# Score units 8 to 12 of a batch issued sooner and in pairs, with the keys' transposes one step earlier

## What is computed

```python
scores = jnp.einsum('bqhd,bkhd->bhqk', q, k) * scale
scores = jnp.where(mask, scores, jnp.finfo(scores.dtype).min)
attn = jax.nn.softmax(scores, axis=-1)
out = jnp.einsum('bhqk,bkhd->bqhd', attn, v).reshape(B, S, N_HEADS * V_DIM)
return out @ Wo
```

## Time and profile before

| | |
|---|---|
| median of 3 runs | 791.5 us (791.44 to 791.93) |
| profiled execution | 791.67 us, span 789.9 us, so 1.77 us lie around the span |
| PE busy | 778.6 us, 99% of the span |
| PE weight loads busy | 711.5 us, 90% |
| DVE busy | 681.7 us, 86% |
| ACT busy | 524.5 us, 66% |
| POOL busy | 479.5 us, 61% |

### The profile page before, as it was taken

One profiled execution on the slowest core, in us unless ns is written; L12 is line 12 of the kernel. 1 busy time (PEld: TensorE's weight loads), 2 busy tenths in 40 slices (PEclk: granted clock), 3 DMA queues, 4 the chain that ended last, 5 costly groups with the idle time before them and its releaser, 6 DMA issues.

```text
span 789.9 us, 23152 instructions
## 1 busy us (share of the span) xinstructions
PE 778.6 (99%) x7976; PEld 711.5 (90%) x7976; DVE 681.7 (86%) x2616; ACT 524.5 (66%) x1612; POOL 479.5 (61%) x1278
## 2 busy tenths in 40 slices
PE   9999999999999999999999999999999999999988
PEld 7889889888889889898998989899898998989867
DVE  6998897888688899989898998989989898998885
ACT  5554454445555787777767777677777867777682
POOL 6880202202236696776867768686776867768673
PEclk9999999999999999999999999999999999999999
DMA  8600220000002222322222322223222222322220
GB/s 302 253 2 2 62 82 27 1 1 1 1 15 52 40 46 52 61 54 36 48 46 50 64 39 50 40 46 55 56 55 35 48 46 49 63 39 53 34 52 28
DMA packets 101334, 41.15 MB, mean 52 GB/s; under 512 B 91744, under 2 KB 98400, under 8 KB 100576
## 3 DMA queue, kind: packets, MB, share of 16 engines
q1 hardware_dynamic: 98896, 38.89, 22.1%
q10 hardware_dynamic: 2320, 0.79, 0.4%
HBM read 14.47 MB, written 4.19 MB: 24 GB/s over the span
## 4 chain that ended last, share of the span: by engine, by line
PE 92%; DVE 4%; ACT 1%; POOL 1%; issue 1%; ACTq 0%; POOLq 0%; DVEq 0%
PE bank L549 63%; PE bank L773 11%; PE bank L795 8%; PE bank L766 3%; PE bank L629 2%; PE bank L815 1%; PE bank L566 1%; DVE SM L1608 1%; PE bank L681 1%; ACT SM L1065 1%; DVE PT L1631 1%; PE bank L641 1%; PE bank L655 1%; POOL SM L2051 1%; PE bank L700 0%
## 5 line engine op out<-in xcount | busy, mean ns | idle before, releaser
L1065 ACT ACTIVATE SM<-SM,stb 128x224 f32<-128x224 f32 (+7 forms) x512 | 207.2, 407 | 62.7 <-DVE stb L1608 58.2
L2051 POOL TENSOR_SCALAR SM<-SM,stb 128x224 f32<-128x224 f32 (+7 forms) x512 | 195.2, 396 | 67.5 <-DVE stb L1615 66.1
L549 PE MATMUL bank<-yh,wq_lo 128*128 128x256 f32 x512 | 150.6, 294 | 0.0
L549 PE MATMUL bank<-yh,wq_hi 128*128 128x256 f32 x512 | 144.7, 283 | 0.0
L549 PE MATMUL bank<-yl,wq_hi 128*128 128x256 f32 x512 | 144.6, 282 | 0.0
L773 PE MATMUL bank<-KT,QT 128*128 128x192 f32 (+4 forms) x640 | 120.9, 327 | 1.7 <-DVE stb L1608 1.7
L1608 DVE CUSTOM_DVE_ANT_0 SM<-bank,CONST 128x224 f32<-128x224 f32 (+3 forms) x320 | 97.2, 348 | 23.3 <-PE bank L773 20.9
L1631 DVE STREAM_TRANSPOSE PT<-SM 128x128 f32<-128x128 f32 (+2 forms) x232 | 99.7, 462 | 16.7 <-PE bank L795 16.7
L773 PEld LDWEIGHTS bank<-KT,QT 128*128 128x128 f32 x640 | 97.5, 190 | 5.3 <-DVE stb L1608 3.6
L549 PEld LDWEIGHTS bank<-yh,wq_lo 128*128 128x128 f32 x512 | 97.1, 190 | 1.4
L549 PEld LDWEIGHTS bank<-yh,wq_hi 128*128 128x128 f32 x512 | 97.1, 190 | 0.0
(11 more groups left out here) (229 smaller groups left out, 2068.9 us busy)
## 6 DMA issues: line engine op xcount, KB each, us to landing
QT<-QA SPq DMA_DIRECT2D x240, 64.0 KB, 2.1
PT<-KV SPq DMA_DIRECT2D x256, 16.0 KB, 1.8
out<-fo SPq DMA_DIRECT2D x32, 128.0 KB, 2.0
X<-in_x SPq DMA_DIRECT2D x7, 512.0 KB, 11.5
stage<-in_wqn SPq DMA_DIRECT2D x2, 1024.0 KB, 5.3
stage<-in_wo SPq DMA_DIRECT2D x2, 1024.0 KB, 4.9
stage<-in_w1t SPq DMA_DIRECT2D x4, 256.0 KB, 5.0
stage<-in_w2t SPq DMA_DIRECT2D x2, 512.0 KB, 6.2
```

The source lines that it names most:

```text
L549: i = e.matmul(dst, a, b, start=(first and j == 0), stop=(last and j == 2), skip_group_check=skip)
L1065: i = e.activation(M[:, at], M[:, at], ACT.Exp, bias=S[:, 0, j:j + 1], scale=-1.0, accum_out=S[:, 1, j:j + 1])
L2051: i = e.tensor_scalar(P[:, at], P[:, at], S[:, 2, j:j + 1], 1.0, ALU.mult, ALU.mult)
```

## The change

TK_AT becomes 7, with TK_FIRST = 8 kept for batch 0. So `l1_tk` and `keys` run one step sooner in batches 1 to 14, and tk moves in the list of shared banks: it now stands ahead of the second output product instead of behind the gate product.

A new function, `scores_at`, gives the units that PE issues at a step. In batches 1 to 14: S7 and S8 at m = 7, S9 and S10 at m = 8, S11 and S12 at m = 9 (in batch 14 only S11), and then nothing at m = 0, 1, 2 of the next batch (in the last batch nothing at 0 and 1). All units still go out in the same order, to the same two banks, with the same waits. `l1_misc` moves ahead of the scores of its step in batches 1 and later. DVE, ACT and POOL keep their steps, but for `keys`.

```diff
-TURN_AT, TM_AT, TK_AT, LORA_AT, MISC_AT = 6, 6, 8, 8, (8, 9)
+TURN_AT, TM_AT, TK_AT, TK_FIRST, LORA_AT, MISC_AT = 6, 6, 7, 8, 8, (8, 9)
+def scores_at(n):
+    if not 0 <= n < TOTAL:
+        return ()
+    b, m = divmod(n, UNITS)
+    if b and m < 3 and b > 1 and (b < NB - 1 or m < 2):
+        return ()
+    if b and b < NB - 1 and m > 6:
+        return {7: (n, n + 1), 8: (n + 1, n + 2), 9: (n + 2, n + 3) if b < NB - 2 else (n + 2,)}[m]
+    if n and with_next(n - 1):
+        return ()
+    return (n, n + 1) if with_next(n) else (n,)
+def tk_of(n):
+    b, m = divmod(n, UNITS)
+    return b + 1 if m == (TK_AT if b else TK_FIRST) and b + 1 < NB else None
 # shared_bank_order
-        if m == TK_AT and b + 1 < NB:
-            js.append(("tk", b + 1))
+        if tk_of(n):
+            js.append(("tk", tk_of(n)))
 # PE's program
-                if n < TOTAL and not (n and with_next(n - 1)):
-                    l1_s(n)
-                    if with_next(n):
-                        l1_s(n + 1)
-                if m == TK_AT and b + 1 < NB:
-                    free_shared("tk", b + 1)
-                    l1_tk(b + 1, jof("tk", b + 1))
+                if m in MISC_AT and 0 < b and b + 2 < NB:
+                    i = 2 * (b + 2) + MISC_AT.index(m)
+                    free_shared("mi", i)
+                    l1_misc(b + 2, i % 2, jof("mi", i))
+                for i in scores_at(n):
+                    l1_s(i)
+                if tk_of(n):
+                    free_shared("tk", tk_of(n))
+                    l1_tk(tk_of(n), jof("tk", tk_of(n)))
 # ACT's program
-                c, i = divmod(n - 1, UNITS)
-                if 0 <= c < NB - 1 and i == TK_AT:
-                    keys(c + 1, jof("tk", c + 1))
+                if n and tk_of(n - 1):
+                    keys(tk_of(n - 1), jof("tk", tk_of(n - 1)))
```

More of the change, by code:

```diff
@@ L913, in _ @@
                     l1_turn(b + 2, jof("ty", b + 2))
-                if m in MISC_AT and b + 2 < NB:
-                    i = 2 * (b + 2) + MISC_AT.index(m)
+                if n in MISC_AT:
+                    i = 4 + MISC_AT.index(m)
                     free_shared("mi", i)
-                    l1_misc(b + 2, i % 2, jof("mi", i))
+                    l1_misc(2, i % 2, jof("mi", i))
                 if m == TM_AT and b + 1 < NB:
```

## The result

The changed kernel takes **802.5 us** (median of four runs, 801.99 to 804.17), the kernel before 791.5 us beside it (791.34 to 791.93). The ratio is 1.0137, 95% interval 1.0125 to 1.0149: slower by 11.0 us between the medians (10.6 between the profiled executions, 802.23 and 791.67). The forecast was 802.3 us in a range of 797.5 to 806.5.

A forecast was written before the change was run, and what follows sets the result against it. PE's own stream was taken to bound batches 1 to 13. Per batch 0.66 + 0.17 + 0.05 = 0.88 us, 11.4 in 13 batches, less 0.3 for pairing and 0.3 at the end: 10.8, so 802.3 us, range 797.5 to 806.5.

The forecast's parts named there:

- Where PE's idle time would come up: 13 PE waits at the second output product's first matmul, each 0.5 to 0.7 us, put down to DVE's rotation.
- The bank wait: Second output product reuses query product 5's bank, so PE waits for DVE's turn_queries: 0.66 us a batch, batches 1 to 13.
- The rule of the Trainium skill on weight loads pulled ahead: Output product's 0.19 us weight load done ahead of its wait would make the total 2.5 us lower; trace spoke against it.
- S10 behind the gate product: S10 needs most(8), which stands behind gate_sum on DVE; PE starts it late and slower: 0.17 us a batch.
- S12: S12, behind the query products, needs most(10) and PE's weights are due slightly sooner: 0.05 us a batch, 0 to 0.3.
- S8: S8 directly behind S7 needs most(6), ready 0.06 us before its weight load: no wait, range 0 to 0.15 us.
- Pairing: Two fewer changes between fp32 scores and fp32r products on PE gain 0.02 us a batch, 0.3 us in all.
- rival 3: Faster: each stop for scores costs an extra 0.13 us, so two fewer in 13 batches give 788.1 us; chance 0.06.
- The end: From S149 in batch 14 the chain runs through ACT and DVE; 0.3 us of gain, 0 to 1.0.
- Rival 1: Waits spread to S8 or S12, up to 0.3 us more a batch, 806.2 us; chance 0.13.
- Rival 2: No wait, no gain: bank released in time, PE's stream only reordered, 791.2 us; chance 0.08.
- the closing line: Chances by outcome: slower 0.88, within 0.2% 0.06, faster 0.06; the forecaster's own case 0.73.

The follow-up runs named there:

- Experiment 1: The changed kernel, but tk keeps its old place in the list of shared banks, behind the gate product; 793.65 us, ratio 1.0025.
- experiment 2: The changed kernel with tk at its old place in the list of shared banks and gate_sum behind most in DVE's step; 791.36 us, ratio 0.9996.
- experiment 5: The changed kernel with gate_sum behind most in DVE's step, tk left where the change put it; 800.27 us, ratio 1.0103.
- experiment 7: The kernel before with one more stop for scores in batches 1 to 14, S3 between two query products; 792.0 us, ratio 0.9999.
- Experiment 8: The kernel before with POOL's residual addition moved behind its normalise in each step; 792.7 us, taken once.

## Why the prediction was right, step by step

- **Where PE's idle time would come up.** Right. 13 waits at the first matmul of the output product, put down to the rotation (0.63 us in the list of loads, within the 0.5 to 0.7 that was named; the matmuls' own list has only 0.39); the batch 34.79 us where 34.80 was forecast; DVE's wait ahead of the attention sums' transposition 1.29 us against 1.30.
- **The bank wait**, forecast 0.66 us (0.58 to 0.75). Experiment 1 takes it away alone: 0.675. The release came 0.06 us after the rotation's end, as taken from the earlier trace rows. The rule of the Trainium skill on weight loads pulled ahead (its page "TensorE: Matmul & The Clock Gate", section "Step-by-step: what each phase is for"), weighed in the prediction, would have made the time 2.5 us lower than forecast; the trace shows the load at 478.78 beginning with its matmul, behind the wait. A load that itself waits was not pulled ahead here either.
- **S10 behind the gate product**, forecast 0.17 us (0 to 0.35). Experiments 2 and 5 give 0.221 and 0.226. Mis-sized by 0.05 us, 0.7 us in all. DVE's statistics start at 484.65 and end at 485.31 + 0.08 = 485.39, 0.74 us, just as forecast; S10's load starts at 485.50, 0.11 us behind that end, where the term had 0.06 from the earlier trace rows. Why this signal took 0.05 longer than the two others I can't say.
- **S12**, forecast 0.05 us (0 to 0.3). None came. The step that failed was the interval from most(8) to most(9), which was put at 3.02 us: weigh took 0.71 us in it instead of 1.27, and most(9) started at 487.12 - 484.65 = 2.47 us behind most(8), 0.55 sooner. PE's first load of S12 then had some 0.5 us in hand, where the forecast saw it 0.08 late.
- **S8**, forecast no wait with 0.06 us in hand. Right: S7 and S8 take the 1.63 us of an M and a W unit without a wait, and with all other waits gone the batch of experiment 2 is shorter than before, so none is left over for S8.
- **Pairing**, forecast 0.02 us a batch. Measured 0.025 in experiment 2, with the transposes and `l1_misc` at their new places. The sum 1.63 = 0.82 + 0.81 in the earlier trace rows was a sound ground to reject rival 3.
- **The end**, forecast 0.3 us of gain. From the first matmul of the T units of batch 14 to that of batch 15 it takes 20.50 us instead of 20.78 (20.50 in experiments 1 and 2 too). In batch 15 a wait of 0.27 us ahead of a score unit is gone, and the attention sums start 10.58 us later than before, while batch 14 started 11.01 later. So 0.43 us, with a different part in it than the one argued: the chain behind 750.90 was advanced by little.
- **The total.** 13 batches gave 11.3 us; less 0.43, and less some 0.3 us by which layer 1's first scores start sooner (262.48 instead of 262.74, in a part whose order isn't changed; over the ten traces this start lies between 262.48 and 263.01, so it is scatter): about the 10.5 us by which the span grew. The forecast had 11.4 - 0.3 - 0.3 = 10.8. It hit 802.3 against 802.5 partly by luck: S10 was 0.05 too small and S12 0.05 too large, which cancel, and the four runs of the changed kernel spread over 2.2 us, far more than the 0.2 us of the miss.
- **The rivals.** Rival 1 (waits spread) needed a wait at S8 or 0.3 us at S12; both pairs show none, 1.63 us each. Rival 2 (no wait) is refuted by the 13 waits; it had a chance of 0.08, while the closing line gives 0.06 to a time within 0.2%, where its 791.2 us would lie, so these two don't agree. Rival 3 (0.13 us a stop) is refuted by experiments 2 and 7.

What stays open: the gain of the change without its waits, 0.3 us in the repeated batches and about as much at the end (20.50 for 20.78), is below what the runs can tell (experiment 2's interval reaches from 1.0 us faster to 0.3 us slower), so no version was found that beats the kernel before.

## What to carry to other kernels

When an order of work is advanced in a kernel whose buffers are handed out in turn from one list, more jobs than the moved one get another predecessor. Here tk went two places ahead, past the output product and the gate product. These two moved back by one, and the jobs six places behind the three got new predecessors as well; all others kept theirs. In the kernel before it was the gate product that stood six places behind query product 5, late enough not to wait; the move gave that place to the output product. Write down for each such job who frees its buffer, and when, before asking what the move gains. The price of such a wait is the difference of two times that both stand in the trace of before, and it is paid in full where the waiting engine has no idle time. And read the distance between starts rather than busy time: here one wait of 0.65 us showed as 0.39, another of 0.2 not at all in the matmuls' brackets, and the busy time rose with them.

## What the runs showed of the hardware

One DVE instruction, weigh, with two inputs in SBUF, 128 x 512, took 0.71 us in one kernel and 1.27 in the other. The timelines of POOL in both, first before:

```profile
481.01 0.73 POOL L2113 TENSOR_TENSOR fo<-fo,X 128x256 f32<-128x256 f32 x1
481.73 1.65 POOL L2051 TENSOR_SCALAR SM<-SM,stb 128x128 f32<-128x128 f32 x3
```

and after:

```profile
485.91 1.58 POOL L2074 TENSOR_SCALAR SM<-SM,stb 128x128 f32<-128x128 f32 x3
487.46 0.73 POOL L2136 TENSOR_TENSOR fo<-fo,X 128x256 f32<-128x256 f32 x1
```

Before, weigh starts at 481.17, 0.16 us into POOL's addition, which ends at 481.74, and weigh ends at 482.44, 0.70 us later: its whole own time. It seems to have stood until POOL's instruction was through. Experiment 8 has the same sum with another instruction of POOL:

```profile
481.95 0.39 POOL L2051 TENSOR_SCALAR SM<-SM,stb 128x128 f32<-128x128 f32 x1
482.14 0.91 DVE L1561 SCALAR_TENSOR_TENSOR w1b<-w1b,PT 128x512 f32<-128x512 f32 x1 [0.33 <-ACT w1b L1059]
```

POOL's ends at 482.34 and weigh at 483.05, 0.71 later. The other way round, of the 1.65 us of POOL's next group before one instruction, begun 0.55 us after weigh, took 0.87 and the two others 0.39 and 0.42, so it was held up by some 0.47 us. After, weigh starts at 486.48 and takes 0.71, and POOL's last instruction of the group of 485.91, begun 0.15 us after it, took 0.86 us. But the one ahead of it had begun before weigh:

```profile
486.26 0.40 POOL L2074 TENSOR_SCALAR SM<-SM,stb 128x160 f32<-128x160 f32 x1
```

By the profile it ran until 486.66, 0.18 us into weigh, and weigh was not longer for it. The Trainium skill describes such a contention: its page "SBUF — State Buffer", section "Who interferes with whom", says that a DVE instruction with two SBUF inputs contends with a GpSimd instruction that reads SBUF, and that the order of issue decides who blocks. The trace agrees in the kernel before and in experiment 8, where weigh ended 0.70 and 0.71 us after the POOL instruction that had begun first. The POOL instruction at 486.26 in the changed kernel does not fit, unless its true end lies before the drawn one; that stays open. Experiment 8 shows that POOL's order sets weigh's time; that an exclusion is the way in which it does was read from these starts and ends, not tried apart.

Two smaller ones: a switch between fp32 scores and fp32r products costs PE 0.010 to 0.012 us, although the first fp32r matmul behind it stands 0.25 to 0.31 us from the second (491.50 to 491.75 and 486.23 to 486.54, both in the changed kernel); and a result of DVE reached PE 0.06 us after the instruction's end at the bank wait, and 0.11 at S10.
